# Two-layer graph network: SyncE fetches one tile of each super group row by row, and the next logits are transposed ahead of the last group

## What is computed

```
edge_index = [src, dst]                      # dst sorted
# layer 0
h   = leaky([x[dst], x[src] - x[dst]] @ W1 + b1, 0.01)
h   = leaky(h @ W2 + b2, 0.01)
x   = layernorm(x + segment_sum(h, dst))
# layer 1, with a loop edge for every node
y      = (x @ W).reshape(N, 4, 64)
logits = leaky(a_src[src] + a_dst[dst], 0.2)
ex     = exp(logits - segment_max(logits, dst)[dst])
alpha  = ex / segment_sum(ex, dst)[dst]
x      = layernorm(x + mean over heads of segment_sum(y[src] * alpha, dst) + bias)
```

## Time and profile before

| | us |
|---|---|
| median of the runs, lowest, highest | 8309.39, 8294.4, 8319.42 (3 runs) |
| the profiled execution's own time | 8288.93 |
| its span | 8287.2 |
| granted TensorE clock, mean | 0.861 |
| layer 0, first gather to last | 94.7 to 4013.6 |
| layer 1, first gather to last | 4102.3 to 8060.3 |

### The profile page before, as it was taken

One profiled execution on the slowest core, in us unless ns is written; L12 is line 12 of the kernel. 1 busy time (PEld: TensorE's weight loads), 2 busy tenths in 40 slices (PEclk: granted clock), 3 DMA queues, 4 the chain that ended last, 5 costly groups with the idle time before them and its releaser, 6 DMA issues.

```text
span 8287.2 us, 208340 instructions
## 1 busy us (share of the span) xinstructions
PE 6139.9 (74%) x46847; PEld 4678.3 (56%) x46848; DVE 5688.8 (69%) x13862; ACT 3827.2 (46%) x9600; POOL 5969.4 (72%) x6281
## 2 busy tenths in 40 slices
PE   6778777777787777877557776767776776777677
PEld 5556555555565555555435555555555555555556
DVE  5555555555555555555568888888888888888887
ACT  4444444444444444444334444444444444444443
POOL 4777777777777777777477777777777777777760
PEclk8898999998988998999678888888888888888887
DMA  4111111111111111111211111111111111111120
GB/s 110 40 40 40 40 40 40 40 40 40 40 40 40 40 40 40 40 40 40 37 30 31 30 31 31 30 31 30 31 30 31 30 31 31 30 31 30 31 28 16
DMA packets 277253, 303.41 MB, mean 37 GB/s; under 512 B 169655, under 2 KB 173252, under 8 KB 276710
## 3 DMA queue, kind: packets, MB, share of 16 engines
q0 software_dynamic: 200704, 265.33, 17.3%
q1 hardware_dynamic: 74450, 34.52, 1.7%
q10 hardware_dynamic: 2068, 3.20, 0.1%
HBM read 286.33 MB, written 16.30 MB: 37 GB/s over the span
## 4 chain that ended last, share of the span: by engine, by line
POOL 37%; issue 24%; PE 19%; DVE 12%; DVEq 3%; POOLq 2%; DMA 1%; ACT 0%; SPq 0%; ACTq 0%
POOL big L427 37%; PE pu L1017 14%; DVE Y L729 2%; POOLq L418 2%; DVE ps L696 1%; DVE rowD L701 1%; DVE S L531 1%; DVE state L755 1%; PE ps L1040 1%; PE ps L997 1%; PE ps L1003 1%; DVEq L280 1%; DVEq L768 1%; PE ps L1029 1%; PE ps L1005 0%
## 5 line engine op out<-in xcount | busy, mean ns | idle before, releaser
L427 POOL DMA_INDIRECT big<-x_dram,idx x3136 | 3003.7, 958 | 1043.0 <-issue 1031.5
L427 POOL DMA_INDIRECT big<-q_dram,idx x3136 | 2964.6, 945 | 1048.0 <-issue 1048.0
L1017 PE MATMUL pu<-Y,S 128*128 128x265 f32 x7872 | 2342.4, 446 | 765.4 <-issue 548.7
L1017 PEld LDWEIGHTS pu<-Y,S 128*128 128x128 f32 x7872 | 1610.2, 215 | 1116.2 <-issue 833.3
L729 DVE TENSOR_TENSOR Y<-big,ps 128x1040 f32<-128x1040 f32 x984 | 1214.5, 1234 | 256.8 <-PE pu L1017 165.0
L531 DVE TENSOR_TENSOR S<-ps,few 128x1024 f32 x978 | 1197.9, 1225 | 150.0 <-DVE few L526 108.6
L571 DVE TENSOR_TENSOR ps<-ps,rowX 128x512 f32<-128x512 f32 x491 | 343.6, 700 | 1371.4 <-ACT rowX L1147 1371.4
L1136 ACT COPY ST<-ps 128x1024 bf16<-128x1024 bf16 x489 | 494.9, 1012 | 1312.8 <-PE ps L906 1312.8
L920 PE MATMUL pu<-rowX,S 128*128 128x192 bf16 x3936 | 561.7, 271 | 495.5 <-SPq L349 454.1
L920 PEld LDWEIGHTS pu<-rowX,S 128*128 x3936 | 383.7, 100 | 651.6 <-issue 564.7
L1219 ACT COPY ST<-ps 128x1024 bf16<-128x1024 bf16 x490 | 495.6, 1011 | 551.0 <-PE ps L1040 551.0
(11 more groups left out here) (179 smaller groups left out, 8468.9 us busy)
## 6 DMA issues: line engine op xcount, KB each, us to landing
big<-q_dram,idx POOLq DMA_INDIRECT x3136
big<-x_dram,idx POOLq DMA_INDIRECT x3136
rowX<-flag_dram SPq DMA_DIRECT2D x196, 32.0 KB
x_dram<-big SPq DMA_DIRECT2D x7, 483.0 KB, 6.4
idx<-srcT_dram SPq DMA_DIRECT2D x98, 32.0 KB, 1.8
dstc<-dstT_dram SPq DMA_DIRECT2D x98, 32.0 KB
q_dram<-state SPq DMA_DIRECT2D x2, 1536.0 KB, 9.7
out<-big SPq DMA_DIRECT2D x6, 448.0 KB
```

Source lines behind the costliest of these rows:

```text
L427: nc.gpsimd.indirect_dma_start(o, None, x_dram if l else q_dram, bass.IndirectOffsetOnAxis(ap=idx[:, half, t:t + 1], axis=0)).then_inc(gat ...
L1017: last = t_.matmul(bank, Sf[:, t, :], Y[:, t, :], start=(t == 0), stop=(t == 7))
```

## The change

Of every super group one tile is no longer gathered by POOL: the last tile in layer 0 (not in the last super group), the first in layer 1. SP loads its 128 source numbers into one partition of rowD, reads them eight at a time into registers, and issues a DMA for each row. In layer 0 the rows are issued in portions of 24 or 16 ahead of the signals of groups 0 to 6, and the signal of the last group waits for them; the chunk of the next super group is asked for after group 1. In layer 1 they are issued in one go after the indices, once the buffer's step is past. SP also waits for x_dram before layer 1's first chunk.

In layer 1, DVE's and PE's loops over the groups become a loop over seven and one by itself. Between them DVE waits for the next super group's gathers and copies its logits (one instruction) and flags, and PE transposes the logits. The boundary keeps the scans; the transposes back go half by half, into ps[4], and three DVE instructions write edgeM and edgeE.

```diff
+LENT = (TS - 1, 0)
+LOAD = 8
-        rowD = sb("rowD", [32, GE], i32)
+        rowD = sb("rowD", [P, GE], i32)
...
+            def steps(self, l, i, turn, arrive=None, between=None):
+
+                apart(self.eng)
+                with self.eng.Fori(0, GS if between is None else GS - 1) as r:
+                    self.group(l, i, r, turn, arrive)
+                if between is not None:
+                    between()
+                    apart(self.eng)
+                    self.group(l, i, GS - 1, turn, arrive)
...
+            numbers = [rowD[32:33, k * P:(k + 1) * P] for k in range(2)]
+            picked = [sp.alloc_register(f"row{j}") for j in range(LOAD)]
+
+            def row_numbers(l, i, half):
+                sp.dma_start(numbers[half], src[ds(i * GE * GS + LENT[l] * P, P)].rearrange("(a e) -> a e", a=1)
+                             ).then_inc(row_no[half], 16)
+
+            def buffer_free(l, i):
+                r = LENT[l] // TG
+                gone = sp.value_load(Bt[0:1, ds(i * GS + r, 1)], min_val=0, max_val=NB - 1)
+                sp.wait_ge(L[l]["y1" if l else "z1"], sp.snap(i * GS + gone + (r + PAST - AHEAD)))
+
+            def fetch_rows(l, half, lo, hi):
+                for a in range(lo, hi, LOAD):
+                    sp.reg_load(picked, numbers[half][:, a:a + LOAD])
+                    for j in range(LOAD):
+                        row = sp.snap(picked[j], min_val=0, max_val=N - 1)
+                        o = (g1 if l else g0r)[a + j:a + j + 1, half * TS + LENT[l], :]
+                        sp.dma_start(o, (x_dram if l else q_dram)[ds(row, 1), :]).then_inc(rows_here[l][half][j % 2], 16)
+
+            ROWCUT = [min(P, LOAD * -(-P * r // (LOAD * (GS - 1)))) for r in range(GS)]
-            def landed(q, half):
+            def landed(i, q, half, more, lent):
                 apart(sp)
+                n = TG
+                if lent:
+                    buffer_free(0, i)
+                    sp.wait_ge(row_no[half], q * 16 + 16)
+                    apart(sp)
                 for r in range(GS):
-                    sp.wait_ge(slot[half][r], q * (16 * TG) + 16 * TG)
+                    if lent and r < GS - 1:
+                        fetch_rows(0, half, ROWCUT[r], ROWCUT[r + 1])
+                    if lent and r == GS - 1:
+                        for a in range(2):
+                            sp.wait_ge(rows_here[0][half][a], q * (8 * P) + 8 * P)
+                        n = TG - 1
+                    sp.wait_ge(slot[half][r], q * (16 * (TG if r < GS - 1 else TG - 1)) + 16 * n)
                     sp.sem_inc(ready, 1)
+                    if r == 1 and more:
+                        chunk(0, i + 1, 1 - half)
+                        row_numbers(0, i + 1, 1 - half) if more > 1 else None
                 sp.sem_inc(gdone, 1)
...
             def chunk1(i, q, half):
-                chunk(1, i, half)
-
-                sp.wait_ge(sgv, i * 4 + 1)
+                sp.wait_ge(gdone, i + (NS + 1))
+                sp.dma_start(idx[:, half, :], srcT_dram[:, ds(i * TS, TS)]).then_inc(idx_in[half], 16)
+                if not (isinstance(i, int) and i == NS - 1):
+                    row_numbers(1, i + 1, 1 - half)
+                buffer_free(1, i)
+                sp.wait_ge(row_no[half], q * 16 + 16 * (NS // 2 + 1))
+                apart(sp)
+                fetch_rows(1, half, 0, P)
+                sp.wait_ge(fredge_flatd, i + (NS + 1))
+                sp.dma_start(dstc[:, half, :], dstT_dram[:, ds(i * TS, TS)]).then_inc(dst_in[half], 16)
+                sp.wait_ge(sgv, i * 5 + 1)
...
             sp.wait_ge(s["flag_out"], 32)
+            sp.wait_ge(x_out, 16 * NCH)
...
+                        lent = LENT[l] if l or not (isinstance(i, int) and i == NS - 1) else TS
                         for t in range(r * TG, r * TG + TG):
+                            if t == lent:
+                                continue
...
+            def arrived(i, q, half):
+                dve.wait_ge(gath[half], q * (16 * (TS - 1)) + 16 * (TS - 1))
+                for a in range(2):
+                    dve.wait_ge(rows_here[1][half][a], q * (8 * P) + 8 * P)
+                dve.sem_inc(gdone, 1)
+                gt = g1[:, half * TS:(half + 1) * TS, D + 1:XW].rearrange("p (g j) h -> p j h g", j=TG)
+                v.tensor_copy(edgeA[:, :, :].rearrange("p j (h g) -> p j h g", h=H), gt).then_inc(sgv, 1)
+                dve.wait_ge(row_in, i * (16 * H) + 16 * H)
+                v.tensor_scalar(rowF[0:GS, :], rowR[0:GS, 1:GE + 1], -1.0, None, ALU.is_lt).then_inc(sgv, 1)
...
+                walk1.steps(1, i, turn1(half), between=None if last else lambda: arrived(i + 1, q + half, 1 - half))
...
+            def turn_maxima(i):
+                rowM = rowD[0:32, :].bitcast(f32)
+                pe.wait_ge(sgv, i * 5 + 4)
+                apart(pe)
                 for j in range(TG):
-                    t_.transpose(ps[3][:, j * 32:j * 32 + 32], rowM[:, j * P:(j + 1) * P], ident[0:32, 0:32])
-                for j in range(TG):
-                    last = t_.transpose(ps[3][:, 256 + j * GS:256 + j * GS + GS],
-                                        rowF[0:GS, j * P:(j + 1) * P], ident[0:GS, 0:GS])
+                    t_.transpose(ps[4][:, 256 + j * GS:256 + j * GS + GS],
+                                 rowF[0:GS, j * P:(j + 1) * P], ident[0:GS, 0:GS])
+                for h in (1, 0):
+                    if h == 0:
+                        pe.wait_ge(sgv, i * 5 + 5)
+                        apart(pe)
+                    for j in range(h * 4, h * 4 + 4):
+                        last = t_.transpose(ps[4][:, j * 32:j * 32 + 32], rowM[:, j * P:(j + 1) * P], ident[0:32, 0:32])
                 last.then_inc(sgp, 1)
```

More of the change, by code:

```diff
@@ L167, in build @@
         ready = sem("ready")
+        row_no = [sem(f"row_no{k}") for k in range(2)]
+        rows_here = [[[sem(f"rows{l}{p}{a}") for a in range(2)] for p in range(2)] for l in range(2)]
         row_in = sem("row_in")
@@ L267, in block, with group @@
                 return self.eng.value_load(Bt[0:1, ds(at, 1)], min_val=0, max_val=NB - 1)
-            def steps(self, l, i, turn, arrive=None):
+            def group(self, l, i, r, turn, arrive):
                 eng = self.eng
[L272 to L285, removed]
+                g = i * GS + r
+                b0 = eng.snap(self.first, min_val=0, max_val=NB - 1)
+                b1 = eng.snap(self.last, min_val=0, max_val=NB - 1)
+                if arrive is not None:
+                    arrive(g)
+                    apart(eng)
+                with eng.Fori(b0, b1 + 1) as b:
+                    k = Turn(eng, l, eng.snap(g + b), r, b)
+                    k.peek = lambda: eng.reg_mov(self.ahead, self.block(g + (AHEAD + 2)))
+                    turn(k)
+                eng.reg_mov(self.first, b1)
+                eng.reg_mov(self.last, self.ahead)
+            def steps(self, l, i, turn, arrive=None, between=None):
[6 more added lines that the diff above has]
+                    self.group(l, i, GS - 1, turn, arrive)
         @block.sync
@@ L353, in _ @@
                 chunk(0, i, i)
+                row_numbers(0, i, i)
             sp.wait_ge(s["flag"], 1)
             sp.dma_start(flag_dram[0:E].rearrange("(p c) -> p c", p=P), edges[:, 0:FLAGS]).then_inc(s["flag_out"], 16)
[L356 to L363, removed]
+            sp.wait_ge(s["q_out"], 16 * (len(QCUT) - 1))
+            landed(0, 0, 0, 0, True)
+            with sp.Fori(0, (NS - 3) // 2) as q:
+                landed(q * 2 + 1, q, 1, 2, True)
+                landed(q * 2 + 2, q + 1, 0, 2, True)
+            landed(NS - 2, (NS - 2) // 2, 1, 1, True)
+            row_numbers(1, 0, 0)
+            landed(NS - 1, (NS - 1) // 2, 0, 0, False)
             for c in range(NCH):
@@ L809, in steps1 @@
             def steps1(i, q, half):
-                maxima(i, q, half)
+                maxima(i, half)
                 dve.wait_ge(dst_in[half], (q + 1 + (NS - NS // 2 if half == 0 else NS // 2)) * 16)
-                walk1.steps(1, i, turn1(half))
+                last = isinstance(i, int) and i == NS - 1
+                walk1.steps(1, i, turn1(half), between=None if last else lambda: arrived(i + 1, q + half, 1 - half))
                 dve.sem_inc(fredge_flatd, 1)
+            arrived(0, 0, 0)
             supers(dve, steps1)
@@ L989, in _, with turn_logits @@
                 last.then_inc(tab1["m"], 1)
-            def turns(i):
-                pe.wait_ge(sgv, i * 4 + 2)
+            def turn_logits(i):
+                pe.wait_ge(sgv, i * 5 + 2)
                 apart(pe)
@@ L1047, in steps1 @@
             def steps1(i, q, half):
-                turns(i)
-                walk1.steps(1, i, turn)
+                turn_maxima(i)
+                walk1.steps(1, i, turn, between=None if isinstance(i, int) and i == NS - 1 else lambda: turn_logits(i + 1))
             prime(pe, 1, "stp ad U0 U1")
             pe.wait_ge(clean, 2)
```

(1 more changed line is left out.)

43 lines of the change are left out of this document (15 added, 28 removed).

## The result

The changed kernel takes 8193.56 us (median of 4 runs, 8190.21 to 8206.81), the kernel before 8306.83 us (4 runs): ratio 0.9872, interval 0.9859 to 0.9884. The prediction said 8180, range 8140 to 9000. The profiled execution took 8190.21 us, its span is 8188.4, 98.8 less than the 8287.2 of before.

A forecast was written before the change was run, and what follows sets the result against it. POOL's gathers were taken to bound layer 0, and two chains of equal pace, gathers and turns with boundary, layer 1. Terms -60 - 62 + 2 - 8 = -128 took the profiled 8288.9 to 8161; 20 us on top gave 8180, range 8140 to 9000.

The forecast's parts named there:

- layer 0, 48 gathers fewer: Layer 0: 48 super groups each save one POOL gather of 1.250 us, -60 us, at POOL's pace.
- SyncE waits for x_dram: Between the layers: waiting for x_dram before asking for layer 1's first indices makes POOL begin about 2 us later.
- layer 1, 49 gathers fewer: Layer 1: 49 gathers fewer at 1.2625 us each, -62 us, if the chain of steps with the boundary follows.
- from the last gather to the end: Layer 1's end: last gather's end to the last super group's first weighting takes 20.1 us instead of 28.3, -8.
- The row price: SyncE's time per fetched row in both layers: 0.52 us, between 0.43 and 0.92, hidden behind POOL's gathers.
- Eight neighbouring words look more like one read than like eight: SyncE's load of eight registers: assumed to cost about one read, 0.05 us a row.
- The rule of 0.2 us for every further register: SyncE's register loads: about 200 ns per register even in bulk, giving 0.685 us a row and 9436 us in all.
- Boundary and order of bounds: Layer 1: boundary 14.1 to 8.4 us, 2.1 added ahead of the last group; steps fall to 77.2, under POOL's 79.5.
- The rival with SyncE as the bound: Both layers: the row loop outlasts POOL's 63 gathers, so the kernel gets slower, +690 to +4070 us; chance 0.35.
- 49 x (128c + ...): Time over before if SyncE bounds both layers, c being us per row: no gain left at c = 0.595.

The follow-up runs named there:

- e2: Kernel before with only layer 1's new boundary, all 64 gathers on POOL and no rows on SyncE: 12144 us, 0.973 of the kernel before.

## Why the prediction was right

| term | forecast | measured |
|---|---|---|
| layer 0, 48 gathers fewer | -60 | -62.4 |
| SyncE waits for x_dram | +2 | +3.5 |
| layer 1, 49 gathers fewer | -62 | -26.1 |
| from the last gather to the end | -8 | -13.4 |
| sum | -128 | -98.8 by the spans |

**The row price** was the unknown on which the sign hung, and 0.52 was right (0.53) by parts that missed both ways: the DMA with its move 0.33 instead of 0.384, the address 0.085 (0.09), an eighth of the load and what comes with it 0.11 instead of 0.05. With 0.048 and 0.063 us a row of room the two layers hid it. "Eight neighbouring words look more like one read than like eight" is now shown: 0.782 against 0.493 for one. The rule of 0.2 us for every further register would have given 0.29 + 7 x 0.2 = 1.69 for eight, and 9436. What the prediction quotes for it from the Trainium skill ("Runtime: NRT & Kernel Launch", Instruction fetch mechanics) does not hold for these loads from SBUF.

**Boundary and order of bounds**: 7.9 and 1.2 against 8.4 and 2.1, DVE waiting in every super group, POOL late next. Right.

**The number is nearer than the mechanism.** The spans fell by 98.8 us where the sum said 128: the profiled execution takes 8190, and 8161 was forecast for it. The 8180 came from adding the 20 us that lay between the profiled execution and the median before; now only 3 lie between them. That one miss covers half of the other is luck.

**The mis-sized term is layer 1's -62.** The prediction multiplied 49 gathers by the pace of before, 1.2625, and took its 0.0125 over layer 0's 1.250 for a constant of layer 1. It was a sum of collisions with DVE's instructions, the updates above all, whose number depends on how the turns stand to the gathers; starting each last group on a gather's landing moved them into the worst place. That this is what moved them is read from the traces of before and after, not from a run that changes it alone on this chip. At 1.274 the remaining 3087 gathers lose 36 us of the 62.

**The tail is right for the wrong reasons, by luck.** 20.1 us were forecast from the last gather's end to the last super group's first weighting; it is 8003.89 - 7975.85 = 28.0, no better than before (28.3). The landing takes 7.2 instead of 1.6 (the padding), which ahead of the last group is newly on the path, and that group 12.1 instead of 8. The gain came after the last weighting: 129.9 us to the end in the kernel before (8287.2 - 8157.3), 114.1 now (8188.4 - 8074.3), less 2.7 lost between the first and last weighting of that super group. Busy time by stretch, of before and of after (us; PE, PEld, DVE, ACT, POOL; PEclk; DMA share, GB/s):

```profile
8165.00:8287.00 122.00, 98.24 (x588) 95.72 (x588) 76.37 (x114) 36.78 (x64) 0.00 (x0) 0.66 0.11 27
```
```profile
8075.00:8188.40 113.40, 86.77 (x604) 83.20 (x602) 80.29 (x132) 39.42 (x77) 0.00 (x0) 0.77 0.12 30
```

The granted clock of this stretch is 0.66 before and 0.77 after, a mixture of the levels 1.2 and 2.4 GHz, with much the same work. From the last weighting to the end, 604 matmuls in both, it is 0.68 before and 0.77 after; PE is busy 102.1 and 87.1 us, DVE 81.6 and 81.0. PE's 15 us are nearly all of the 15.8 gained there, with the granted clock as the difference that the rows show. That the clock followed from the change is not shown; nothing in the change touches this code.

**The rival with SyncE as the bound** (0.35) lost here by 0.05 us a row, and held in every run with rows on the other chips (1.045 to 1.186 with the load of eight), through a mechanism it did not name: not a dearer row, but rows and gathers that cannot run side by side. The prediction's sum, 49 x (128c + ...), sees none of it, since it assumed that SyncE's instructions cost the same beside POOL's as alone.

## What to carry to other kernels

Work moved to an idle engine's queue is free only while both queues run side by side, and that can differ from one chip or occasion to the next (0.987 here, 1.18 there): measure such a change on more than one chip, and compare the new instructions' durations while the other engine works and while it pauses. Here a pace that lay a few ns over the bare one was a count of collisions, and a change that started one engine on the other's landings moved that count. Two things are worth a trial where gathers set the pace, though no run here shows the time they give back: one operand of DVE's updates in PSUM, and different numbers as padding of an index list.

## What the runs showed of the hardware

- A load of registers from SBUF on SyncE takes 0.493 us for one, 0.727 for two and 0.782 for eight; a DMA of one row with its address in a register 0.225 us of the queue's time, 0.53 with everything around it.
- An indirect gather that starts 0.04 to 0.29 us after a DVE update with two inputs in SBUF (0.42 us long) ends as if it had started 0.29 us after that update's start; with one of the inputs in PSUM it isn't held up at all, and DVE is no slower. A copy of 128x256 f32 from SBUF to SBUF (0.40 us) holds up a gather that started 0.11 to 0.19 us ahead of it: 1.22 to 1.31 us instead of 0.945.
- On four of five chips 58 to 66% of the steps between instructions of SyncE's queue are 0.70 or 1.40 us while GpSimd gathers by indices, and instructions 0.04 to 0.23 us long follow each other at once while it pauses. PE is hit too, without any row on SyncE. From e2's timeline, weight loads of one line one after the other:

```profile
2408.01 0.19 PEld L1010 LDWEIGHTS pu<-edgeE,rowA 128*128 128x128 f32 x1 [0.88 <-issue]
2408.77 0.19 PEld L1010 LDWEIGHTS pu<-edgeE,rowA 128*128 128x128 f32 x1 [0.58 <-issue]
2409.50 0.19 PEld L1010 LDWEIGHTS pu<-edgeE,rowA 128*128 128x128 f32 x1 [0.55 <-issue]
```

- They start 0.73 to 0.76 us apart; on the first chip such loads follow within 0.12. In the whole of e2, 645 of 2129 loads of this line that start while a gather runs or within 2 us after it come over 0.5 us behind the one before, and none of the 1301 others. This is likely part of why the kernel before takes 1.5 times as long there; no trace of it was taken on those chips, so its share is open.
- Where gathers of 128 rows that all name one row of a table in DRAM follow each other, most packets of eight rows take 1.3 to 1.9 us where different rows take 0.2, and the last packet ends 5 to 7.5 us after the last gather instead of 1.1 to 1.3.
